# Transposes of x, of the first and of the last two heads' probabilities taken from TensorE to VectorE and HBM, and other warm-ups

## The reference

```
q = layernorm(x) @ Wq;  k = ctx @ Wk;  v = ctx @ Wv          # (1024, 512) @ (512, 32 * 128)
score = einsum('bqhd,bkhd->bhqk', q, k) / sqrt(128) + bias   # 16 batches, 32 heads, 64 x 64 each
probs = softmax(where(mask, score, -inf)) * mask
x = x + einsum('bhqk,bkhd->bqhd', probs, v) @ Wo             # (1024, 4096) @ (4096, 512)
n = layernorm(x)
x = x + n @ base_W.T + base_b + 2 * sum over 8 experts of (n @ A[e].T) * w[e] @ B[e].T
```

## Time and profile before

| | |
|---|---|
| time, median of 3 runs | 775.98 us (775.21 to 776.94) |
| the profiled execution's time, and its span | 777.37 us, 775.5 us |
| PE busy | 766.0 us, 99% |
| DVE, ACT, POOL busy | 541.8 us (70%), 384.8 us (50%), 196.6 us (25%) |
| mean granted TensorE clock | 0.999 |
| chain that ended last | PE 94%, DVE 3%, issue 1%, ACT 1% |
| DMA | 133.05 MB, 172 GB/s |

### The profile page before, as it was taken

How to read it: one execution, slowest core, us unless ns; L and a number is a source line. 1 busy time by engine, 2 the same in 40 slices (tenths; PEclk the granted TensorE clock), 3 DMA queues, 4 the chain that set the end, 5 groups by cost and what they waited for, 6 DMA issues and landing times.

```text
span 775.5 us, 16682 instructions
## 1 busy us (share of the span) xinstructions
PE 766.0 (99%) x6272; PEld 639.1 (82%) x6272; DVE 541.8 (70%) x979; ACT 384.8 (50%) x1110; POOL 196.6 (25%) x203
## 2 busy tenths in 40 slices
PE   9999999999999999999999999999999999999998
PEld 7888888888888888887888888888888888888886
DVE  5874626257677676578778877887678767867974
ACT  5662526245555464475654465435543565426510
POOL 0224041014424433323132312232122313010300
PEclk9999999999999999999999999999999999999999
DMA  6536673244565456577766777556756666541002
GB/s 231 203 123 217 220 244 137 109 140 160 163 190 164 164 163 187 167 235 217 229 181 209 226 208 208 170 176 205 201 165 197 201 188 196 154 148 57 1 15 95
DMA packets 128236, 133.05 MB, mean 172 GB/s; under 512 B 46479, under 2 KB 93583, under 8 KB 128158
## 3 DMA queue, kind: packets, MB, share of 16 engines
q1 hardware_dynamic: 128158, 132.00, 54.3%
HBM read 88.98 MB, written 42.99 MB: 170 GB/s over the span
## 4 chain that ended last, share of the span: by engine, by line
PE 94%; DVE 3%; issue 1%; ACT 1%; DMA 0%; ACTq 0%
PE pY L1452 43%; PE pP L1452 40%; PE pY L1613 4%; PE pO L1649 2%; PE pT_ L1649 1%; PE pO L1452 1%; DVE y L1167 1%; ACT pr L798 1%; PE pS L1649 1%; DVE st L1018 1%; PE pO L1501 0%; PE pS L1501 0%; DVE wk_lo L948 0%; PE pY L1528 0%; DVE wo_lo L948 0%
## 5 line engine op out<-in xcount | busy, mean ns | idle before, releaser
L798 ACT ACTIVATE pr<-pr,mx 128x64 f32<-128x64 f32 x256 | 86.2, 343 | 68.0 <-DVE mx L1187 68.0
L1452 PE MATMUL pY<-wo_hi,oT_hi 128*128 128x512 f32 x248 | 97.3, 392 | 0.3 <-DVE y L1167 0.2
L1452 PE MATMUL pY<-wo_lo,oT_hi 128*128 128x512 f32 x248 | 96.6, 389 | 0.0
L1452 PE MATMUL pY<-wo_hi,oT_lo 128*128 128x512 f32 x248 | 96.5, 389 | 0.0
L1167 DVE TENSOR_TENSOR y<-y,pY 128x512 f32<-128x512 f32 x124 | 83.9, 676 | 15.2 <-PE pY L1452 14.1
L690 ACT CAST wk_hi<-twk 128x256 fp32r<-128x256 f32 x128 | 50.7, 408 | 65.2 <-PE pP L1452 53.4
L948 DVE TENSOR_TENSOR wk_lo<-wk_raw,wk_hi 128x256 fp32r<-128x256 f32 x96 | 48.5, 506 | 46.5 <-ACT wk_hi L690 45.1
L1452 PE MATMUL pP<-xo_hi,wk_hi 128*128 128x512 f32 x196 | 77.9, 398 | 0.0
L1452 PE MATMUL pP<-xo_lo,wk_hi 128*128 128x512 f32 x196 | 76.4, 390 | 0.0
L1452 PE MATMUL pP<-xo_hi,wk_lo 128*128 128x512 f32 x196 | 76.4, 390 | 0.0
L623 POOL TENSOR_TENSOR bias<-bias,madd 128x512 f32<-128x512 f32 x32 | 41.3, 1306 | 137.6 <-DMA bias<-in_fside_Bx32xSxS 137.5
(11 more groups left out here) (283 smaller groups left out, 1862.2 us busy)
## 6 DMA issues: line engine op xcount, KB each, us to landing
v_hbm<-stage SPq DMA_DIRECT2D x64, 256.0 KB, 2.1
k_hbm<-stage SPq DMA_DIRECT2D x64, 256.0 KB, 3.7
k<-k_hbm SPq DMA_DIRECT2D x16, 1024.0 KB, 6.4
v<-v_hbm SPq DMA_DIRECT2D x16, 1024.0 KB, 7.2
wk_raw<-in_L_xattn_Wk SPq DMA_DIRECT2D x16, 512.0 KB, 4.6
wo_raw<-in_L_xattn_Wo SPq DMA_DIRECT2D x16, 512.0 KB, 3.7
bias<-in_fside_Bx32xSxS SPq DMA_DIRECT2D x128, 64.0 KB, 3.6
wk_raw<-in_L_xattn_Wq SPq DMA_DIRECT2D x16, 512.0 KB, 4.6
```

Of the source, the lines that this page charges most:

```text
L798: nc.scalar.activation(pr[s][:, b, :], pr[s][:, b, :], ACT.Exp, bias=mx[:, s, b:b + 1], accum_out=sm[:, s, b:b + 1]).then_inc(exp_made, 1)
L1452: mm = nc.tensor.matmul(bank_, a, b, start=first and n == 0, stop=last and n == len(terms) - 1, skip_group_check=read_between)
```

## The change

What it does, on each engine:

1. Warm-ups: the 8 transposes of 128x128 ahead of the first tile of ctx become 4 of 128x128 and 44 of 32x32, and the 26 of 32x32 ahead of the second tile become 40.
2. x: the 32 transposes of the four x pairs leave PE. DVE normalises one block earlier and transposes the two tiles of a pair by blocks of 32x32 (`xb`); SP stores them (`x_out`, 2 DMAs of 256 KB) and loads them back with 8 DMAs of 64 KB (`x_back`) straight into `first_x` and `low_x`, from which ACT and DVE read. ACT's copy `rows_out` goes.
3. Heads 0, 1, 30 and 31 go by blocks as the others do: `turn_p` leaves PE and `turned_p` leaves ACT; `turn_blocks`, `store_p` and `load_p` are added. For the first pair DVE inverts each head's sums by itself (`invert_first`).
4. In iterations 3, 7 and 11 of the main loop product 1 of the Q block stands between the two `times_v` instead of behind them.
5. In the last pair two `split_ffn` stand one `add_tile` later on DVE.

The diff, cut to its core (left out: buffer addresses, semaphores, the forms of the operands of the x pairs, wait counts that change since no head is treated apart):

```diff
@@ -436,6 +457,24 @@
                              ).then_inc(ld_wk[w % 2], 16)
+            def x_out(j):
+                for i in range(2):
+                    sp.wait_ge(xb_made, 2 * j + i + 1)
+                    sp.dma_start(x_hbm[2 * j + i], xb[:, i, :, :].rearrange("p a n -> p (a n)")).then_inc(put_x[i], 16)
+            def x_back(j):
+                if j >= 1:
+                    sp.wait_ge(sum_step, 4 * (4 + j))
+                    sp.wait_ge(a01_lo, 4 + j)
+                    sp.wait_ge(a6_lo, 4 + j)
+                for i, dst in enumerate((first_x, low[1])):
+                    sp.wait_ge(put_x[i], 16 * (j + 1))
+                    blocks = x_hbm[2 * j + i].rearrange("(t k) (a n) -> a k t n", t=4, a=4)
+                    for a in range(4):
+                        sp.dma_start(dst[32 * a:32 * a + 32, :, :], blocks[a]).then_inc(ld_xt[i], 16)
             def load_bias(h):
@@ -495,10 +535,14 @@
                     load_wk(n - 10)
+                if 17 <= n < 29 and n % 3 == 2:
+                    x_out((n - 17) // 3)
...
                     store(n - 1, 2, c21_made)
+                if 17 <= n < 29 and n % 3 == 2:
+                    x_back((n - 17) // 3)
                 if n != Q0:
@@ -536,6 +580,10 @@
             load_wk(QA - 9)
+            store_p(0)
+            store_p(1)
+            load_p(0)
+            load_p(1)
             sp.wait_ge(wo_l, 1)
@@ -691,9 +738,11 @@
             def first_high(j):
-                act.wait_ge(turned, FIRST_TURN[j] + 1)
-                nc.scalar.copy(a_part(j, 0)[:, 0:2, :, tile_cols(j)],
-                               first_turn(j)[:, :].rearrange("p (k c t) -> p k c t", k=2, c=2)).then_inc(a01_hi, 1)
+                if j < 4:
+                    act.wait_ge(turned, FIRST_TURN[j] + 1)
+                else:
+                    act.wait_ge(ld_xt[0], 64 * (j - 3))
+                nc.scalar.copy(like(j, a01_of(j, 0)), first_of(j)).then_inc(a01_hi, 1)
             def rows_out(j):
@@ -871,9 +912,6 @@
                 h = 2 * i
-                if i == 0:
-                    turned_p(h)
-                    turned_p(h + 1)
                 exp(h + 2, 0)
@@ -909,8 +947,6 @@
             wo_high(NP - 1)
-            turned_p(h + 2)
-            turned_p(h + 3)
             split_ffn(4)
@@ -1047,13 +1086,21 @@
                 for m, t in ((2 * n, n), (2 * n + 1, n + 4)):
-                    b = m % NX
+                    b, i = m % NX, m % 2
                     dve.wait_ge(rstd_made, m + 1)
-                    if m >= NX:
-                        dve.wait_ge(turned, 8 + m - NX + 1)
-                    nc.vector.tensor_scalar(xn[:, b, :], y[:, t, :], mv[:, b, 0:1], rstd[:, b:b + 1],
+                    if m >= 2:
+                        dve.wait_ge(xb_made, m - 1)
+                    nc.vector.tensor_scalar(xn[:, i, :], y[:, t, :], mv[:, b, 0:1], rstd[:, b:b + 1],
                                             ALU.subtract, ALU.mult).then_inc(xn_made, 1)
+                for i in range(2):
+                    m = 2 * n + i
+                    dve.wait_ge(xn_made, m + 1)
+                    if n >= 1:
+                        dve.wait_ge(put_x[i], 16 * n)
+                    nc.vector.transpose(xb[:, i, :, :].rearrange("p g (c q) -> p c g q", c=DC),
+                                        xn[:, i, :].rearrange("p (c g q) -> p c g q", c=DC, g=4)).then_inc(xb_made, 1)
             def first_t3():
@@ -1142,10 +1189,10 @@
                     nc.vector.tensor_reduce(some[:, :], mask8[:, :, :], AX.X, ALU.max).then_inc(msk, 1)
+                if 15 <= n < 27 and n % 3 == 0:
+                    moments_of_x((n - 15) // 3)
                 if 16 <= n < 28 and n % 3 == 1:
-                    moments_of_x((n - 16) // 3)
-                if 17 <= n < 29 and n % 3 == 2:
-                    normalise((n - 17) // 3)
+                    normalise((n - 16) // 3)
             def split_ffn(n):
@@ -1248,12 +1300,15 @@
             lower_w(w2, 0)
+            invert_first(0)
+            weights(0)
+            turn_blocks(0)
+            invert_first(1)
+            weights(1)
+            turn_blocks(1)
+            make_c22(QB)
...
             lower_w(w2, 2)
-            invert(0)
-            weights(0)
-            make_c22(QB)
-            weights(1)
             lower_w(w2, 3)
@@ -1328,12 +1383,14 @@
             weights(h + 2)
+            turn_blocks(h + 2)
...
             weights(h + 3)
+            turn_blocks(h + 3)
+            add_tile(i, 4)
             split_ffn(2)
-            add_tile(i, 4)
+            add_tile(i, 5)
             split_ffn(3)
-            add_tile(i, 5)
             add_tile(i, 6)
@@ -1509,18 +1566,10 @@
                     pe.wait_ge(kept0_made, 2)
-                elif j == 4:
-                    pe.wait_ge(as_lo, 4)
...
                     pe.wait_ge(a6_lo, j - 1)
-                if j < 4:
-                    turn_ctx(j, first_turn(j))
-                    turn_ctx(j + 4, second_turn(j))
-                else:
-                    m = 2 * (j - 4)
-                    pe.wait_ge(xn_made, m + 2)
-                    turn(xn[:, m % NX, :], first_turn(j))
-                    turn(xn[:, (m + 1) % NX, :], second_turn(j))
+                turn_ctx(j, first_turn(j))
+                turn_ctx(j + 4, second_turn(j))
             def warm_up(count, n=P):
@@ -1540,11 +1589,12 @@
                        for c in range(2)]
-            warm_up(8)
+            warm_up(4)
+            warm_up(44, 32)
...
             warm_up(12)
-            warm_up(26, 32)
+            warm_up(40, 32)
             turn_ctx(1, first_turn(1))
@@ -1585,8 +1635,6 @@
                 times(n - 1, 4)
-                if prep_at(n) is not None:
-                    turn_pair(prep_at(n))
                 times(n, 6)
@@ -1720,14 +1754,15 @@
                 h = 2 * i
-                if i == 0:
-                    turn_p(h)
-                    turn_p(h + 1)
...
                 times_v(h)
+                products = [1, 2, 6, 7] if i else [2, 6, 7]
+                if i % 4 == 3:
+                    times(n, products.pop(0))
                 times_v(h + 1)
-                for p in (1, 2, 6, 7) if i else (2, 6, 7):
+                for p in products:
                     times(n, p)
@@ -1754,8 +1789,6 @@
                 times_wo(i, t)
-            turn_p(h + 2)
-            turn_p(h + 3)
             ffn_weights(4)```

PE at the program's start, before (the names are the PSUM tile written and what is multiplied; `ident` is the identity):

```order
L1528 MATMUL pY<-ident 128x128 x8
L1501 MATMUL pS<-ident,ctx 128x128 x4
L1528 MATMUL pY<-ident 128x128 x12
L1528 MATMUL pY<-ident 32x32 x26
L1501 MATMUL pO<-ident,ctx 128x128 x4
L1452 MATMUL pP<-wv_hi,co_hi 128x512
```

More of the change, by code:

```diff
@@ L209, in xattn_ffn @@
         sums_a = [at("sums_c", R2 + 2048, [P, 4, 2, P]), at("sums_x", R4 + 8192, [P, 4, 2, P])]
+        first_x = at("first_x", R4 + 14336, [P, 4, P])
         kept0 = [at("kept0_a", R2 + 6144, [P, 2, 2, P]), at("kept0_b", R2 + 8192, [P, DC, P])]
@@ L351, in raw_block, with first_of, second_of, like @@
             return raw[:, 2 * r:2 * r + 2, c * width:(c + 1) * width]
+        def first_of(j):
+            if j < 4:
+                return first_turn(j)[:, :].rearrange("p (c t) -> p c t", c=DC)
+            return first_x[:, :, :].rearrange("p t (c q) -> p c t q", c=DC)
+        def second_of(j):
+            if j < 4:
+                return second_turn(j)[:, :].rearrange("p (c t) -> p c t", c=DC)
+            return low[1][:, :, :].rearrange("p t (c q) -> p c t q", c=DC)
+        def like(j, a):
+            return a if j < 4 else a.rearrange("p c (t q) -> p c t q", t=4)
         def tw_of(w):
@@ L366, in tile_cols, with a01_of @@
             return slice(j % 4 * P, (j % 4 + 1) * P)
+        def a01_of(j, part):
+            return a_part(j, part)[:, 0:2, :, tile_cols(j)].rearrange("p k c t -> p (k c) t")
         def piece(n, i):
@@ L394, in next_set, with steps_before @@
             return wset(n + 1) if n + 1 < NBLK and wset(n + 1) != wset(n) else None
-        def by_blocks(h):
-            return 2 <= h < H - 2
-        def turned_before(h):
-            return min(h, 2) + max(h - (H - 2), 0)
+        def steps_before(m):
+            return 4 * m + (2 if m else 0)
         def late_set(n):
@@ L981, in last_low @@
                 dve.wait_ge(a6_hi, j + 1)
-                lower(a_part(j, 1)[:, 6, :, cols], second_turn(j)[:, 2 * P:4 * P].rearrange("p (c t) -> p c t", c=2),
-                      a_part(j, 0)[:, 6, :, cols], a6_lo)
+                lower(like(j, a_part(j, 1)[:, 6, :, cols]), second_of(j)[:, 2:4],
+                      like(j, a_part(j, 0)[:, 6, :, cols]), a6_lo)
             def sums_of_a(j):
-                low_, s, k = low[j // 4], sums_a[j // 4], SUM_ORDER.index(j)
-                one = first_turn(j)[:, :].rearrange("p (k c t) -> p k c t", k=2, c=2)
+                s, k = sums_a[j // 4], SUM_ORDER.index(j)
```

(32 more changed lines are left out.)

93 lines of the change are left out of this document (39 added, 54 removed).

## The result

The changed kernel takes 780.43 us (median of 8 executions, 777.93 to 782.77), the kernel before 776.76 in the same comparison: a ratio of 1.0045, 95% interval 1.0032 to 1.0058. Slower, where 773.5 us and most probably faster was forecast. The profiled execution took 780.75 us with a span of 779.0, 3.5 more than before.

What follows compares the result with a forecast made beforehand. PE was taken to bound the kernel, busy 766.0 of 775.5 us. Terms 0.9 - 3.5 - 3.5 - 0.4 + 3.7 + 0.3 = -2.5 us took 777.37 to 774.9, the median to 773.5; range 770.7 to 777.4.

Steps and rivals of the forecast that it cites:

- The start: Warm-ups ahead of ctx: first transpose 1.1 us late, half recovered, and more small ones behind; +0.9 us, ends 0 and +1.8.
- x pairs: Blocks with x pairs: PE loses 8 transposes worth 0.87 us, four times; -3.5 us, ends -2.0 and -3.7.
- The cover: x's way through HBM: loads there at 186.2, 189.3 at worst; a late pair costs ACT up to 1.8 us, PE nothing.
- The moved product: Iterations 3, 7 and 11: six long matmuls give late code time to arrive; -3.5 us, ends 0 and -3.5.
- the shift by 24 instructions: Main loop: code edges come some 24 instructions earlier, helping iterations 4 and 8; -0.4 us, ends +1.0 and -1.8.
- the third rival: Pieces at code edges stay, being something else or the code coming no earlier: -3.9 falls away, 777.4 us; chance 0.14.
- The first pair: Heads 0 and 1: PE waits for probabilities through HBM, 4.2 us late, 0.5 back; +3.7 us, ends -0.4 and +5.8.
- the first rival: PE's wait of over 3 us at heads 0 and 1 lowers its clock, costing about 2: 775.5 us; chance 0.24.
- The wait is cut in two by `times_v` of head 0: Heads 0 and 1: argument against a clock fall, which would cost about 2 us.
- The last pair: Heads 30 and 31: PE loses 0.87 us of transposes, the way through HBM takes 8.1; +0.3 us, ends -0.9 and +1.5.

Runs made afterwards that it cites:

- e4: The changed kernel with the old warm-ups (8 large; 12 large and 26 small): 787.8 us, ratio 1.0142 to the kernel before.
- e11: The changed kernel with 15 large transposes as first filler and the moved product in iterations 4, 8, 12: 779.2 us, ratio 1.0035 to the kernel before.
- e1: The changed kernel with 32 unread transposes during PE's first-pair wait and the moved product in iterations 2, 6, 10: 779.5 us, ratio 1.0041 to the kernel before.
- e2: The changed kernel with the first pair's probabilities transposed by PE and copied by ACT as before: 777.95 us, ratio 1.0018 to the kernel before.
- e3: The changed kernel with no moved product, product 1 behind both `times_v` in every iteration: 783.2 us, ratio 1.0076 to the kernel before.
- e9: The changed kernel with the first pair's two stores ahead of the load of weights on SP: 779.7 us, ratio 1.0035 to the kernel before.
- e6: The kernel before with 44 fulfilled waits on PE ahead of the loop, which made 22 instructions: 777.25 us, ratio 1.0004 to the kernel before.
- e12: The kernel before with 88 fulfilled waits on PE ahead of the loop, which made 44 instructions: 781.5 us, ratio 1.0051 to the kernel before.
- e7: The kernel before with the changed kernel's warm-ups, 108 instructions more: 786.3 us, ratio 1.0138 to the kernel before.

## Why the prediction was wrong

**The start: wrong in size, +1.8 for +0.9.** The failing step is "If the clock rises at the same moment as before ... some half, 0.55, remains." It rose 1.4 us later (7.5 for 6.1), and the whole delay remained. e4 shows that the 1.8 is the warm-ups' (first product at 7.8). e11, with large transposes of the same length, had the early rise and 1.1 of it back, in one execution. In two of six profiled kernels with the small filler it rose 6.5 and 9.2 us later again, 1.8 more on the first product.

**x pairs: right in mechanism, -2.45 for -3.5.** PE lost the transposes. The cover was thinner than I said: the stores took 4.6 with weights in front, just beyond my upper bound of 4.5, and what I expected PE "to see nothing" of was 1.0 us in the fourth block. The miss is partly this execution's: in e1, e2, e4 and e11 the same x pairs gave 2.8 to 3.2 with no such wait. What makes the fourth pair late in some executions stays open.

**The moved product: the step that failed outright.** I gave -3.5 to the move and -0.4 to the shift by 24 instructions. By e3 the shift is worth -1.6 and the move -0.3 (-0.8 by e9's loop); e6, which has nearly the same place and no other change, makes the shift -0.9. The mechanism, code that arrives late at the edges of 256 instructions, is shown (e12, e4, and the packets of all traces); two errors were in my use of it. I left out the price of the move: PE goes once more from small to long matmuls and back, 0.43 us each time. And I took the length of a stop at a given place to be fixed, while it follows the start of the packet, 0.3 to 1.9 us. The rule of the Trainium skill that I weighed ("Runtime: NRT & Kernel Launch", "Instruction fetch mechanics": the fetch is mostly hidden) does not hold in this kernel's small matmuls, and the part of the third rival that says the pieces "are something else" is refuted; its other part, that the moved product would bring little, came near.

**The first pair: the wait right, the clock left out.** The stores landed at 346.4 and 347.0 (I placed them at 346.5), and the last load at 351.6 (351.8). My 4.2 us of delay was good, and e2 shows the whole term by taking it away (iteration 0 at 24.0). What failed is that I chose against the first rival, "the wait pulls the clock down": it came true, at about 2 us (e1: 1.76). "The wait is cut in two by `times_v` of head 0" was no argument, as the first part alone was 3.2 us. In this row the rule of the Trainium skill, "TensorE: Matmul & The Clock Gate", section "HAM oscillation — how this bites in real kernels", and the trace agree: 3.2 us without a matmul, and a granted clock of 0.50 behind it.

**The last pair: right in size.** +0.2 in the rest of the span, +0.3 forecast. PE waited 1.1 us there for `pT` (the third row of its waits above). It was not tried apart.

**The sum.** No single rival made the time: +0.9, +1.05, +2.2 and +1.9 beyond forecast in four terms all went one way, 6 us in all. My range took in one such miss at a time.

## What to carry to other kernels

Where an engine works through a long straight program and is 99% busy, the number of instructions ahead of its fastest stretch is a parameter of its own: before a change is judged, compare the stretches that it didn't touch, and try it with a few idle instructions more. A transfer that replaces work of the bounding engine costs its wait plus what the clock does behind the wait; if the wait can't be removed, keep the engine at work during it, as e1 did. Try small stores that someone waits for ahead of large loads, but look which large load really holds them. And before a wait in one profile is explained, look whether other executions of the same code have it: the late fourth pair and the late rise of the clock came in some only.

## What the runs showed of the hardware that was not expected

- 44 more instructions without any work make the loop 3.5 us longer and the kernel 0.5% slower (e12). Over all kernels the loop took 299.5 (e9) to 306.5 us (e7, with 1.7 for the clock). Stops fell at 194 to 196 modulo 256 in all kernels.
- PE went on no sooner than 1.1 us after the 16 KB packet of its code had come, in 14 traces; 60 stops in the loops ended 1.1 to 1.7 us after it.
- Two fulfilled waits on PE made one instruction in the trace: 24, 44, 28 and 88 added 12, 22, 14 and 44.
- After 3.2 us without a matmul the granted clock was 0.50 up to 355.7, 5.9 us beyond the wait. It fell once after 1.9 us too (e7), and not after 1.8 in e4.
- The clock's first rise scatters between kernels, one execution each: 4.7 to 8.0 us, and 14.0 and 16.7 in two.
